# Attention and two convolution layers on one core: one PSUM bank for both accumulations, a fourth bank for the maxima, a ring of 16 probability tiles, and all additions of probabilities on GpSimd

## What is computed

```python
m = jax.image.resize(mask, (B, 1, H, W), method='bilinear')          # 32x32 -> 64x64
q = proj(Wq, bq) / math.sqrt(hd); k = proj(Wk, bk); v = proj(Wv, bv)  # (16, 4096, 32)
attn = jax.nn.softmax(jnp.einsum('bnd,bmd->bnm', q, k), axis=-1)
fuse = jnp.einsum('bnm,bmd->bnd', attn, v)
hybrid = _conv1x1(jnp.concatenate([x, fuse], axis=1), Wf, bf)
x = hybrid * m + x * (1.0 - m)
# second layer: depthwise 3x3, relu, channel gate, 1x1 (fusion), depthwise 3x3, 1x1 (balance), times x
```

## Time and profile before

| | |
|---|---|
| median of three runs | 4200.41 us (4199.91 to 4203.75) |
| the profiled execution's own time | 4203.13 us |
| its span | 4201.3 us |
| TensorE matmul | busy 4044.0 us, 96% |
| TensorE weight load | busy 1975.3 us, 47% |
| VectorE | busy 3550.1 us, 84% |
| ScalarE | busy 2339.9 us, 56% |
| GpSimd | busy 3222.2 us, 77% |

### The profile page before, as it was taken

One profiled execution on the slowest core, in us unless ns is written; L12 is line 12 of the kernel. 1 busy time (PEld: TensorE's weight loads), 2 busy tenths in 40 slices (PEclk: granted clock), 3 DMA queues, 4 the chain that ended last, 5 costly groups with the idle time before them and its releaser, 6 DMA issues. The chain is left out here.

```text
span 4201.3 us, 81722 instructions
## 1 busy us (share of the span) xinstructions
PE 4044.0 (96%) x20341; PEld 1975.3 (47%) x20341; DVE 3550.1 (84%) x5350; ACT 2339.9 (56%) x4424; POOL 3222.2 (77%) x1360
## 2 busy tenths in 40 slices
PE   7979999999999999999999999999999999969797
PEld 4534444444444444444444444444444444424343
DVE  3279999999989999999899999999999999917989
ACT  1216666666656666666566666666666666641213
POOL 2429999999989999999899999999999999960000
PEclk9959999999999999999999999999999999989998
DMA  6931100110001101110111011100110000013021
GB/s 190 285 100 39 41 21 22 42 39 22 21 23 41 31 21 32 41 31 21 31 41 31 21 31 38 35 20 18 40 38 21 21 21 21 17 27 85 20 80 40
DMA packets 213798, 184.92 MB, mean 44 GB/s; under 512 B 115986, under 2 KB 140740, under 8 KB 213316
## 3 DMA queue, kind: packets, MB, share of 16 engines
q1 hardware_dynamic: 213508, 181.74, 16.2%
HBM read 122.10 MB, written 59.24 MB: 43 GB/s over the span
## 5 line engine op out<-in xcount | busy, mean ns | idle before, releaser
L761 ACT ACTIVATE prob<-st 128x512 f32<-128x512 f32 x4096 | 2154.3, 601 | 1309.3 <-PE st L626 1048.6
L819 DVE TENSOR_REDUCE block_max<-mx 128x1 f32<-128x512 f32 x4096 | 2562.0, 683 | 343.4 <-PE mx L633 330.0
L490 POOL TENSOR_TENSOR prob_sum<-prob_sum,prob 128x1024 f32<-128x1024 f32 x768 | 1929.3, 2512 | 127.5 <-POOL prob_sum L490 100.4
L633 PE MATMUL mx<-keys,max_queries 96*128 96x512 f32 x4096 | 1648.0, 426 | 38.2 <-DMA keys<-k_scratch 27.8
L626 PE MATMUL st<-queries,keys 97*128 97x512 f32 x4096 | 1574.5, 411 | 1.6 <-ACT prob L761 1.5
L490 POOL TENSOR_TENSOR prob_sum<-prob 128x1024 f32<-128x1024 f32 x448 | 1067.8, 2383 | 253.1 <-ACT prob L761 253.1
L633 PEld LDWEIGHTS mx<-keys,max_queries 96*128 96x128 f32 x4096 | 777.8, 191 | 737.3 <-DVE block_max L819 564.8
L645 PE MATMUL acc<-prob,values 128*32 128x512 f32 x8192 | 1039.7, 602 | 0.0
L626 PEld LDWEIGHTS st<-queries,keys 97*128 97x128 f32 x4096 | 776.7, 190 | 520.6 <-ACT prob L761 282.2
L645 PEld LDWEIGHTS acc<-prob,values 128*32 128x32 f32 x8192 | 194.4, 108 | 427.1 <-issue 226.1
L665 PE MATMUL dacc<-prob_sum,ones 128*32 128x512 f32 x2048 | 273.0, 605 | 9.2 <-POOL prob_sum L490 9.2
(11 more groups left out here) (119 smaller groups left out, 1213.8 us busy)
## 6 DMA issues: line engine op xcount, KB each, us to landing
max_queries<-q_scratch SPq DMA_DIRECT2D x384, 64.0 KB, 1.9
queries<-q_scratch SPq DMA_DIRECT2D x384, 64.0 KB, 2.0
keys<-k_scratch SPq DMA_DIRECT2D x168, 128.0 KB, 2.5
x<-in_x SPq DMA_DIRECT2D x18, 512.0 KB, 4.1
q_scratch<-high SPq DMA_DIRECT2D x32, 256.0 KB, 4.4
k_scratch<-high SPq DMA_DIRECT2D x16, 512.0 KB, 4.9
q_scratch<-low SPq DMA_DIRECT2D x32, 256.0 KB, 5.0
k_scratch<-low SPq DMA_DIRECT2D x16, 512.0 KB, 4.9
```

The lines of the kernel that those rows point to most:

```text
L490: ops.tensor_tensor(psum[k][:, :, :], a[:, :, :], prob[(first + i) % RING][:, :, :], ALU.add).then_inc(added[own], 1)
L633: nc.tensor.matmul(mx[bank(j, p)][:, :], qm[p][:, h, ns * P:(ns + 1) * P], kk[gp][0:SPLIT, h, blk * CH:(blk + 1) * CH], start=True, stop=T ...
L761: nc.scalar.activation(prob[s % RING][:, h, :], st[bank(i, p)][:, :], ACT.Exp).then_inc(exp_done, 1)
L819: nc.vector.tensor_reduce(bmax[p][:, j // MB, j % MB:j % MB + 1], mx[bank(j, p)][:, :], AX.X, ALU.max).then_inc(mx_taken, 1)
```

## The change

1. The values' accumulation and the sums share one PSUM bank `acc`: all `V` of a unit come first, then all `S`. Between them ScalarE copies both halves of `acc` out (`copy_num`, two copies of 64x512), and after the last `S` it copies all of it (`copy_den`, 128x512). VectorE adds the two halves of the numerator from SBUF; the two halves of the denominator are added only after the way through DRAM, as two columns of 8 (`dsum`).
2. The freed bank becomes a fourth `mx`.
3. The ring has 16 tiles and not 8. The tiles are stored as one tensor `prob`.
4. GpSimd makes all additions: 20 in a unit (19 before, and 3 on VectorE). Their order is woven: a group's first addition stands ahead of the last one of the group before. There are 6 `S` in a unit.
5. `ORDER` is new: 150 letters. The `V` and `S` stand in 10 stretches; before, in 15.
6. `SCORES_AHEAD` is 28 (13), `BLOCKS_AHEAD` 40 (29).
7. To make room in SBUF, `wf`, `fu`, `ba` and `diag` are written to DRAM at the start of projection and loaded again at the start of the image phase; the first mask is upsampled there too, ahead of `mixer`.

```diff
-GROUPS = [4, 4, 4, 4, 3, 3, 4, 4]
-BY_VECTOR = [3]
+GROUPS = [4, 4, 4, 4, 4, 4, 2, 2]
+BY_VECTOR = []
 BANKS = 3
+MAX_BANKS = 4
-RING = 8
+RING = 16
-ORDER = ("msmsmsVmsmsmsmsVsmsmsmsmsmVmsmsmsmsmsVVVsmsmsmssmsmsmsVVsmmsmssSVsmssmmsVV"
-         "mssmsmmssmsmSmssmsmmVmssmsmmVmsmssmmVmmsmssmSmsmsmsmVmssmsmmVSsmsmsmsSsmsms")
-SCORES_AHEAD = 13
-BLOCKS_AHEAD = 29
+ORDER = ("smmsmsmsmsmsVVVVmssmmsmsmsmsmsVVsmsmsmsmsmsmsmsmsVVsmsmsmsmmsmsmVVsmsmsmsms"
+         "msmsmsmVVsmsmsmsmsmsmsmsmVVmsmmsmsmVVsmssmSssmsmmmsSSsmssmmsmsmsmsmsSSSsmsms")
+SCORES_AHEAD = 28
+BLOCKS_AHEAD = 40
-TAKE_NUM, TAKE_DEN, INVERT = 24, 32, 40
-ADD_AFTER = [43, 51, 54]
-NUM_AFTER, DEN_AFTER = 6, 13
-SCALE_AFTER = 4
+TAKE_NUM, INVERT = 24, 49
+ADD_AFTER = []
+NUM_AFTER, DEN_AFTER = 10, 25
+SCALE_AFTER = 11
...
+def chain_order():
+    chains = [k for k, size in enumerate(GROUPS) if k not in BY_VECTOR and size > 1]
+    order = [(k, i) for k in chains for i in range(1, GROUPS[k])]
+    for k, after in zip(chains, chains[1:]):
+        if GROUPS[k] > 2:
+            order.remove((after, 1))
+            order.insert(order.index((k, GROUPS[k] - 1)), (after, 1))
+    return order
...
             def values(u, gp, q):
                 if q == 0:
-                    pe.wait_ge(num_ready, u + 1)
+                    pe.wait_ge(den_ready, u + 1)
...
             def sums(u, i):
                 if i == 0:
-                    pe.wait_ge(den_ready, u + 1)
+                    pe.wait_ge(num_out, 2 * (u + 1))
...
-            def num_half_out(v):
+            def copy_num(v):
                 act.wait_ge(num_ready, v + 1)
                 act.wait_ge(v_done, QUADS * (v + 2))
-                nc.scalar.copy(num_even[:, :], acc[0:2 * HD, :]).then_inc(num_half, 1)
+                for a in range(2):
+                    nc.scalar.copy(num_part[a][:, :], acc[2 * HD * a:2 * HD * (a + 1), :]).then_inc(num_out, 1)
-            def den_half_out(v):
-                act.wait_ge(den_ready, v + 1)
+            def copy_den(v):
+                act.wait_ge(den_stored, 16 * (v + 1))
                 act.wait_ge(sums_done, SUMS * (v + 2))
-                nc.scalar.copy(den_even[:, :], dacc[0:2 * HD, :]).then_inc(den_half, 1)
+                nc.scalar.copy(den[:, :], acc[:, :]).then_inc(den_ready, 1)
...
+            for w in IMAGE_WEIGHTS:
+                sp.dma_start(scratch[w][:, :], flat(keep[w])).then_inc(put_away, 16)
...
-            dve.wait_ge(mask_loaded, 16)
-            upsample(nc, dve, small, keep["mask"], mstep, 0)
-            dve.wait_ge(mstep, NM)
...
+            sp.dma_start(flat(late["wf"]), scratch["wf"][:, :]).then_inc(weights_back, 16)
+            load(0, 0, 0)
+            load_mask(0)
+            load(0, 1, 1)
+            for w in IMAGE_WEIGHTS[1:]:
+                sp.dma_start(flat(late[w]), scratch[w][:, :]).then_inc(weights_back, 16)
...
+            pe.wait_ge(weights_back, 16 * len(IMAGE_WEIGHTS))
             pe.wait_ge(mixer, CT)
...
+            dve.wait_ge(mask_loaded, 16)
+            upsample(nc, dve, small, mask, mstep, 0)
             for t in range(CT):
                 own = keep["wf"][:, t, t * P:(t + 1) * P]
                 nc.vector.tensor_tensor(own, own, keep["ident"][:, :], ALU.subtract).then_inc(mixer, 1)
```

More of the change, by code:

```diff
@@ L421, in attention_phase @@
         qm = [sb(f"max_queries{p}", [SPLIT, 2, CH], F32R) for p in range(2)]
-        prob = [sb(f"prob{r}", [P, 2, CH]) for r in range(RING)]
+        prob = sb("prob", [P, RING, 2, CH])
         psum = [sb(f"prob_sum{r}", [P, 2, CH]) for r in range(len(GROUPS))]
@@ L427, in attention_phase @@
         warm = sb("exp_warm", [P, 1])
-        num_even = sb("num_even", [2 * HD, CH])
-        den_even = sb("den_even", [2 * HD, CH])
+        num_part = [sb(f"num_part{a}", [2 * HD, CH]) for a in range(2)]
         num = sb("num", [2 * HD, CH])
-        den = sb("den", [2 * HD, CH])
-        dcol = sb("den_col", [P, 2 * CH // P])
+        den = sb("den", [P, CH])
+        dcol = sb("den_col", [P, 2, 2 * CH // P])
+        dsum = sb("den_sum", [P, 2 * CH // P])
         rcol = sb("rec_col", [P, 2 * CH // P])
@@ L656, in sums @@
                         pe.wait_ge(added[j in BY_VECTOR], ADDS[j in BY_VECTOR] * (u + 1) + adds_until(j, GROUPS[j] - 1))
-                    src = [psum[k + a] for a in range(2)]
+                    src = [psum[k + a][:, :, :] for a in range(2)]
                 else:
@@ L660, in sums @@
                     pe.wait_ge(exp_done, TILES * (u + 1) + 2 * t + 4)
-                    src = [prob[(t + a) % RING] for a in range(2)]
+                    src = [prob[:, (t + a) % RING, :, :] for a in range(2)]
                 for a in range(2):
@@ L806, in between @@
                         take_num(v - 2)
-                    if j == TAKE_DEN:
-                        take_den(v - 2)
                     if j == INVERT:
                         invert(v - 2)
-                for at, (k, i) in zip(ADD_AFTER, additions):
+                for at, piece in zip(ADD_AFTER, PIECES):
                     if prev and j == at:
-                        add(dve, nc.vector, v - 1, k, i)
+                        add_up(dve, v - 1, *piece)
             def maxima(v, p, prev=True, older=True):
@@ L850, in unit @@
             def unit(u, prev=True):
-                for k, size in enumerate(GROUPS):
-                    if k not in BY_VECTOR:
-                        for i in range(1, size):
-                            add(pool, nc.gpsimd, u, k, i)
-                    if k == SCALE_AFTER and prev:
+                for n, (k, i) in enumerate(CHAINS):
+                    add(pool, u, k, i)
+                    if n == SCALE_AFTER and prev:
                         scale(u - 1)
@@ L880, in image_phase @@
         xf = [sb(f"xf{p}", [P, 2 * CT, CH]) for p in range(2)]
-        mask = keep["mask"]
+        mask = sb("mask", [P, HH, WW])
+        late = image_weights(sb)
+        keep = {**keep, **late}
         small = [sb("m32", [P, 32, 32]), sb("q32", [P, 32, 32]), sb("m64", [P, 32, WW])]
@@ L950, in _ @@
         def _(sp):
-            sp.sem_inc(mask_loaded, 16)
             for p in range(2):
@@ L996, in image @@
                 store(b, NCH // 2, NCH)
-            for p in range(2):
-                load(0, p, p)
+            sp.dma_start(flat(late["wf"]), scratch["wf"][:, :]).then_inc(weights_back, 16)
[4 more added lines that the diff above has]
+                sp.dma_start(flat(late[w]), scratch[w][:, :]).then_inc(weights_back, 16)
             for p in range(2):
@@ L1294, in _, with image_weights @@
             image(B - 1, False)
+def image_weights(sb):
+    late = {w: sb(f"{w}T", [P, kts, ots * P]) for w, ots, kts in WEIGHTS if w in IMAGE_WEIGHTS}
+    late["diag"] = sb("diag", [P, CT, EDGE_PE, P])
+    return late
 def build(nc, dram, out):
@@ L1313, in build @@
         }
-        for w, ots, kts in WEIGHTS:
-            if w not in PROJECTIONS:
-                keep[w] = sb(f"{w}T", [P, kts, ots * P])
         scratch = {
@@ L1329, in build @@
         with ExitStack() as first:
-            weights = {w: first.enter_context(nc.sbuf_tensor(f"{w}T", [P, kts, ots * P], F32))
-                       for w, ots, kts in WEIGHTS if w in PROJECTIONS}
+            early = lambda name, shape: first.enter_context(nc.sbuf_tensor(f"first_{name}", shape, F32))
+            weights = {w: early(f"{w}T", [P, kts, ots * P]) for w, ots, kts in WEIGHTS if w not in IMAGE_WEIGHTS}
+            weights.update(image_weights(early))
             setup_phase(nc, dram, {**keep, **weights})
```

120 lines of the change are left out of this document (64 added, 56 removed).

## The result

| | before | after |
|---|---|---|
| median | 4201.07 us (4 runs, 4199.91 to 4203.75) | 4670.04 us (4 runs, 4666.10 to 4672.24) |
| ratio to before, 95% interval | | 1.1114 (1.1095 to 1.1134) |
| span of the profiled execution | 4201.3 us | 4664.3 us |
| from one row of maxima to the next | 53.64 us | 61.13 us |

The forecast was 4158, with a range from 4128 to 4192. The change costs 469 us instead.

A forecast was written before the change was run, and what follows sets the result against it. TensorE was taken as the bound, with 52.94 of 53.64 us a unit its own work. Units -62.6, beginning +14.2, end -6.5, weights and mask +12.1 sum to -42.8, so 4158 us, range 4128 to 4192.

The forecast's parts named there:

- End: Last unit and what follows: GpSimd's chain ends earlier, -7.8 us; one more S costs about 1.7; sum -6.5 us.
- the four rivals: Alternatives: ScalarE pacing, 0.13; GpSimd as bound, 0.03; late handover, 0.12; stalls of 0.70 with image phase losing 17, 4174 us.
- GpSimd: GpSimd in each unit: 20 additions and one scaling take 50.0 of 52.6 us, weaving hides 0.16 between chained additions; hidden by 10.
- Order and stalls: TensorE in each unit: 52.13 us of work in the new order plus 0.5 of stalls, 52.63; -62.6 us over 62 units.
- that is even, and I count nothing: Shared bank, first S waiting for the numerator copies: 2.36 us left, 2.3 needed; counted 0, bounds 0 and 0.5 a unit.
- the 0.34 that the prediction named as a sign: TensorE at the ends of long stretches: a few steps of 0.34 us were expected, against 0.233 for a plain product.
- Fourth bank: Maxima banks: with VectorE's additions gone, it lets VectorE be one more block behind, 0.61 us or four pairs, removing VectorE's stalls.
- Beginning: Before unit 0: eleven more blocks cost 6.6 us and fifteen more scores 7.6; sum +14.2 us, first score near 303.
- Weights and mask: Projection and image phase: reloads and upsampling the mask in the open at the image phase's start; sum +12.1 us.
- Rival A: Attention units: ScalarE paces the long stretches, losing 0.06 us a pair; at 0.25 a stretch 4236 us; chance 0.13.
- rival B: Attention units: GpSimd becomes the bound; at 2.6 us an addition the unit takes 54.2, the time 4255 us; chance 0.03.
- Rival C: Attention units: a handover, row of maxima or copies, comes late each unit, +0.5 us, so 4189 us; chance 0.12.

The follow-up runs named there:

- e2_unwoven: The changed kernel with GpSimd's chains of additions one after the other instead of woven, `den_sum` left as it is: 4177.91 us, ratio 0.9938.
- e9_spare_one: e1_reduce plus one unused VectorE `tensor_scalar` a unit with one SBUF operand of 128x8, right behind the reciprocal: 4993.61 us, ratio 1.1882.
- e1_reduce: The changed kernel with `den_sum` made by a `tensor_reduce` over one operand instead of a `tensor_tensor` over two: 4149.24 us, ratio 0.987.
- e4_reduce_3banks: e1_reduce with three maxima banks instead of four: 4382.82 us, ratio 1.0432.
- e6_reduce_mixfirst: e1_reduce with VectorE subtracting the identity before upsampling the mask in the image phase, and a separate semaphore for `wf`: 4146.75 us, ratio 0.9868.

## Why the prediction was wrong

**The step that failed** is in *End*: "VectorE's addition of 0.7 goes, a tiny one of 0.3 comes." The tiny one is `den_sum`. I took its price from its size, counted it at the end only, and left it out of the unit's sum, where it comes 64 times. Measured it is 7.5 us, and with what follows from it 8.6 a unit. It was no rival either: the four rivals look at ScalarE, GpSimd's throughput, handovers, and the stalls with the image phase. The same reading failed in *GpSimd*: "The woven order hides the 0.16 between chained additions" was booked as a gain, and e2_unwoven shows that it is these pauses that let VectorE in, 8.2 us a unit (61.13 - 52.98).

**The trace of before had the row.** VectorE's own additions read two SBUF operands too. Their groups by line in the kernel before:

```profile
L490 DVE TENSOR_TENSOR prob_sum<-prob_sum,prob 128x1024 f32<-128x1024 f32 x128 | 263.4, 2058 | 0.6 <-ACT prob L761 0.6
...
L490 DVE TENSOR_TENSOR prob_sum<-prob 128x1024 f32<-128x1024 f32 x64 | 187.5, 2929 | 6.0 <-ACT prob L761 4.4
```

The same operation on the same size takes 2.93 in one place, 2.06 on average in others, and 1.60 in the earlier trace rows. I used only the 1.60. Beside them, in the timeline of the kernel before, three places:

```profile
3660.12 2.38 POOL L490 TENSOR_TENSOR prob_sum<-prob_sum,prob 128x1024 f32<-128x1024 f32 x1 [0.16 <-ACT prob L761]
3660.59 2.99 DVE L490 TENSOR_TENSOR prob_sum<-prob 128x1024 f32<-128x1024 f32 x1
3662.66 3.17 POOL L490 TENSOR_TENSOR prob_sum<-prob_sum,prob 128x1024 f32<-128x1024 f32 x1 [0.16 <-POOL prob_sum L490]
...
3669.84 3.16 POOL L490 TENSOR_TENSOR prob_sum<-prob_sum,prob 128x1024 f32<-128x1024 f32 x1 [0.16 <-POOL prob_sum L490]
3672.97 2.26 POOL L848 TENSOR_TENSOR fuse<-num,fuse 64x512 f32<-64x512 f32 x1
...
3724.51 1.28 POOL L848 TENSOR_TENSOR fuse<-num,fuse 64x512 f32<-64x512 f32 x1
```

VectorE's addition starts at 3660.59 beside one of GpSimd's that ends at 3662.50, and ends itself 1.08 later, at 3663.58. GpSimd's next one starts at 3662.66 and ends at 3665.83, which is 2.38 after 3663.45. So the two took turns: VectorE waited 1.9, worked 1.1 from the pause on, and GpSimd then waited 0.8. The 1.60 of the earlier trace rows holds a wait as well: it starts at 3672.48, GpSimd's addition beside it ends at 3673.00, and it ends itself 1.08 later, at 3674.08. So VectorE's own price is 1.08, and GpSimd's 2.38 is 2.2 times that, not 1.5 times as the prediction has it; its estimate of 3.2 for an addition at 2 times came from the 1.60 and falls with it. I did read that GpSimd's mean was 2.51 "with VectorE's additions beside some of them", but took it as a price on GpSimd's side alone. Asked the other way round, what becomes of VectorE if the pauses of 0.16 aren't there, these rows raise the question that decides the case. They don't give the answer: at 3673.00 VectorE got in although the scaling followed directly, and that it would be passed over three times in a row stands in no row of before. The rule of the Trainium skill on the shared ports, told at e9_spare_one, speaks against exactly this instruction, and the prediction did not weigh it; by its letter it would have warned of the wait, though not of its length.

**The other steps** can be read off e1_reduce, where only the failed one is repaired. It measures 4149.2, the forecast was 4158, inside its range.

- *Order and stalls.* Forecast 52.13 + 0.5 = 52.63, measured 52.57. By position in the order, stalls are 0.3 to 0.4, of which 0.18 is the first S waiting for the two numerator copies ("that is even, and I count nothing"). The 0.5 was booked for ScalarE at the ends of the long stretches, and there the usual step is the plain 0.233, with none of the 0.34 that the prediction named as a sign. So the order came out by its reason, the 0.5 by luck.
- *Fourth bank.* The forecast took it as the reason why VectorE's share of the stalls goes; e4_reduce_3banks puts 3.8 us a unit on it. Right, and larger than I had sized it.
- *Beginning.* First score forecast near 303, measured 301.5; unit 0 starts at 315.2, forecast 317.1.
- *End.* From the start of unit 62 to the end of the last addition 87.0, forecast 88.6.
- *Weights and mask.* From the last addition to the first `mix` 40.5 instead of 24.6, so +15.9, where +14.4 was counted with the longer S. The idle time is ended by VectorE, as forecast.
- *Not foreseen.* At the two places where the loop of units turns over, the rows are 57.4 and 57.2 apart, before 63.5 and 61.5. That is 10 less, or 8 when the shorter period is taken off, and accounts for most of the 9 us by which e1_reduce beats the forecast. I didn't look into why.
- *Rival A*, ScalarE paces the long stretches, and *rival B*, GpSimd is the bound: both fell. *Rival C*, a late handover, is worth the 0.18 above where its price was 0.5; scores wait for the row's DMAs 0.3 us in the whole loop. In e1_reduce GpSimd idles 261.2 us waiting for the first S, 4.2 a unit, more than the 2.6 expected, and 0.96 of the difference is the scaling, which takes 1.27 now instead of the 2.23 of the earlier trace rows. The rule of the Trainium skill that the prediction named ("GPSIMD Engine Reference", section on engine selection: GpSimd about 2 times slower) agrees with the trace by the 2.2 above. The bound that the prediction drew from it did not come, since GpSimd's additions stayed at 2.37 to 2.39 and left it time.

The best version of all is e6_reduce_mixfirst or e1_reduce, which the runs can't tell apart: 1.3% faster than the kernel before, and 11% faster than the change as it was made.

## What to carry to other kernels

Before an engine is tuned to run without gaps, look for instructions on the other engine that get in only because of those gaps: if the same operation on the same shape has different durations at different places in a trace, find out what its neighbour does there before you take the shortest for its price. Price a new small instruction by the nearest row with the same operand places (SBUF or PSUM), not by its size, and count it wherever the loop repeats it. Where VectorE has to work in SBUF beside a steady stream on GpSimd, give it a form that passed here (a reduction, a reciprocal, an operand from PSUM), or leave pauses in the stream, close enough that one stands ahead of whichever instruction is running.
